# Self-attention's product of folded values and turned probabilities, as three products of rounded parts in three of four groups

## The reference

```python
b, sq, _ = x.shape                       # 2, 128; 4 groups of 4 heads, 128 wide
q = jnp.einsum('bsh,he->bse', x, w_q).reshape(b, sq, GROUPS, HPG, KVC)
kv = jnp.einsum('bsh,he->bse', x, w_kv)
k, v = jnp.split(kv, 2, axis=-1)         # one key and one value head a group
scores = jnp.einsum('bqgpd,bkgd->bgqpk', q, k) * (SCALE / LAYER_INDEX)
scores = jnp.where(causal[None, None, :, None, :], scores, -jnp.inf)
probs = jax.nn.softmax(scores, axis=-1).astype(x.dtype)
ctx = jnp.einsum('bgqpk,bkgd->bqgpd', probs, v).reshape(b, sq, HEADS * KVC)
return jnp.einsum('bse,eh->bsh', ctx, w_dense)
```

## Time and profile before

| | |
|---|---|
| Median of 3 runs | 344.44 us (344.17 to 345.36) |
| The profiled execution's own time | 344.5 us |
| Its span, first to last instruction | 342.7 us |
| Granted TensorE clock, mean | 1.000 |
| Busy: PE, DVE | 328.6 us (96%), 270.5 us (79%) |
| Busy: ACT, POOL | 228.9 us (67%), 220.7 us (64%) |

### The profile page before, as it was taken

The page is one execution under the profiler, slowest core; times in us unless marked ns, Lnnn a source line. Parts: engine busy times, 40 slices in busy tenths (PEclk is TensorE's granted clock), DMA queues, the critical chain, the costliest instruction groups (busy, mean ns, idle before and its releaser), DMA issues.

```text
span 342.7 us, 6810 instructions
## 1 busy us (share of the span) xinstructions
PE 328.6 (96%) x2222; PEld 297.3 (87%) x2222; DVE 270.5 (79%) x466; ACT 228.9 (67%) x410; POOL 220.7 (64%) x136
## 2 busy tenths in 40 slices
PE   6999988999999999999999999899999999899995
PEld 5887867999999999999999988899888897699994
DVE  2776888898988989889889889577559746489996
ACT  3799449577687677777777676874155676266771
POOL 3766709799499599499598686924626773117540
PEclk9999999999999999999999999999999999999999
DMA  6811468876886895895875977994043054005630
GB/s 201 253 33 38 91 158 191 207 178 142 224 202 138 204 207 124 208 203 127 204 179 115 202 179 175 212 294 137 2 135 112 0 155 153 4 0 138 175 102 32
DMA packets 32565, 49.98 MB, mean 146 GB/s; under 512 B 5536, under 2 KB 23072, under 8 KB 32544
## 3 DMA queue, kind: packets, MB, share of 16 engines
q1 hardware_dynamic: 32544, 49.72, 57.8%
HBM read 20.08 MB, written 0.26 MB: 59 GB/s over the span
## 4 chain that ended last, share of the span: by engine, by line
PE 81%; DVE 6%; ACT 4%; SPq 3%; issue 2%; POOL 1%; DMA 1%; DVEq 0%; POOLq 0%; ACTq 0%
PE bank L586 12%; PE bank L587 11%; PE bank L588 11%; PE pair L586 10%; PE pair L588 10%; PE pair L587 10%; SPq L284 3%; PE bank L977 2%; PE bank L790 2%; PE bank L1007 1%; ACT probs L1248 1%; PE pair L970 1%; PE bank L970 1%; ACT first_pT L1320 1%; PE pair L936 1%
## 5 line engine op out<-in xcount | busy, mean ns | idle before, releaser
L455 POOL TENSOR_TENSOR pT<-pT,pT_hi 128x1024 fp32r<-128x1024 f32 x54 | 129.5, 2422 | 35.5 <-ACT pT_hi L1258 35.4
L1248 ACT ACTIVATE probs<-probs,lowest 128x2048 f32<-128x2048 f32 x32 | 64.4, 2012 | 23.3 <-DVE lowest L1640 23.3
L1258 ACT ACTIVATE pT_hi<-pT 128x1024 fp32r<-128x1024 f32 x56 | 57.6, 1055 | 13.0 <-DMA pT<-ctx_raw 8.6
L586 PE MATMUL bank<-pT_hi,ctx_lo 128*128 128x256 f32 x224 | 63.9, 285 | 1.2 <-POOL pT L455 1.2
L587 PE MATMUL bank<-pT,ctx_hi 128*128 128x256 f32 x224 | 64.1, 286 | 0.0
L588 PE MATMUL bank<-pT_hi,ctx_hi 128*128 128x256 f32 x224 | 63.5, 284 | 0.0
L586 PE MATMUL pair<-ctxT_hi,qk_lo 128*128 128x512 f32 x128 | 52.2, 408 | 0.0
L588 PE MATMUL pair<-ctxT_hi,qk_hi 128*128 128x512 f32 x128 | 50.1, 391 | 0.0
L587 PE MATMUL pair<-ctxT_lo,qk_hi 128*128 128x512 f32 x128 | 50.0, 391 | 0.0
L1640 DVE CUSTOM_DVE_ANT_0 probs<-pair,mask_bias,lowest 128x1024 f32<-128x1024 f32 x32 | 41.0, 1280 | 10.7 <-PE pair L588 10.1
L455 POOL TENSOR_TENSOR ctx_lo<-ctx_raw,ctx_hi 128x512 fp32r<-128x512 f32 (+1 forms) x19 | 31.4, 1668 | 23.0 <-DVE route L2028 8.5
(11 more groups left out here) (280 smaller groups left out, 793.5 us busy)
## 6 DMA issues: line engine op xcount, KB each, us to landing
pT<-blocks SPq DMA_DIRECT2D x112, 128.0 KB, 2.3
pT<-ctx_raw SPq DMA_DIRECT2D x112, 128.0 KB, 2.3
ctx_raw<-ffn_experts_gate_up_dram SPq DMA_DIRECT2D x16, 256.0 KB, 2.9
wq<-in_L_xattn_Wq_dram SPq DMA_DIRECT2D x8, 256.0 KB, 2.7
ctx_raw<-in_ctx_dram SPq DMA_DIRECT2D x8, 256.0 KB, 6.7
wo<-in_L_xattn_Wo_dram SPq DMA_DIRECT2D x8, 256.0 KB, 2.9
blocks<-in_L_attn_w_dense_dram SPq DMA_DIRECT2D x4, 512.0 KB, 4.9
ctx_raw<-_L_ffn_experts_down_dram SPq DMA_DIRECT2D x16, 128.0 KB, 2.5
```

Source lines behind the costliest of these rows:

```text
L455: pool.tensor_tensor(dst, src, hi.bitcast(F32), ALU.subtract).then_inc(ready, 1)
L586: pe.matmul(dst, w[1], x[0], start=start, stop=False)
L1248: act.activation(probs[:, j], probs[:, j], ACT.Exp, bias=lowest[:, p, j, 1:2], scale=-1.0, accum_out=den[:, p, j:j + 1]).then_inc(exps, 1)
L1258: act.activation(hi_slot(c), chunk(p, c).bitcast(F32), ACT.Copy).then_inc(pT_hi_ready, 1)
```

## The change

In groups 0, 1 and 2 the product of `attend2` is done by `product`, with operands in two parts each. The parts lie in tiles that are not in use at that stage (`p2T`'s in `wq_hi`, `wo_hi`, `wq_lo`, `wo_lo`, `v2`'s in `qT_hi`, `qT_lo`). ACT's copy of the turned probabilities writes the rounded part instead of the float32 tile; a new function `rest_p2T` on DVE subtracts it from PC[b] for the low part. DVE's `copy_v` writes a rounded part, waits for it, and subtracts. `rest_p2T(r - 1, b)` stands in DVE's queue ahead of `scale2(r, b)`. In group 3 the product stays as it was.

```diff
--- before.py
+++ after.py
@@ -175,6 +175,9 @@
         v2 = work[:, 1280:1536].rearrange("p (b d) -> p b d", b=B)
         p2 = work[:, 1536:2560].rearrange("p (b h k) -> p b h k", b=B, h=HR)
         p2T = work[:, 2560:3584].rearrange("p (b n) -> p b n", b=B)
+        p2T_hi = (wq_hi[:].rearrange("p k e -> p (k e)"), wo_hi[:].rearrange("p j n -> p (j n)"))
+        p2T_lo = (wq_lo[:].rearrange("p k e -> p (k e)"), wo_lo[:].rearrange("p j n -> p (j n)"))
+        v2_hi, v2_lo = (v[:, 0:B * P].rearrange("p (b d) -> p b d", b=B) for v in (qT_hi, qT_lo))
         nm2 = work[:, 3584:3592].rearrange("p (b h) -> p b h", b=B)
         ds2 = work[:, 3600:3608].rearrange("p (b h) -> p b h", b=B)
         rd2 = work[:, 3616:3624].rearrange("p (b h) -> p b h", b=B)
@@ -277,6 +280,7 @@
         gu_psum, silu_ready, h_ready, down_psum, added3 = (
             sem("gu_psum"), sem("silu_ready"), sem("h_ready"), sem("down_psum"), sem("added3"))
         stored = sem("stored")
+        p2T_hi_ready, v2_hi_ready = sem("p2T_hi_ready"), sem("v2_hi_ready")
         xn_half, half_stat = sem("xn_half"), sem("half_stat")
 
         def move(eng, p, a, q):
@@ -974,7 +978,11 @@
             def attend2(r, b):
                 pe.wait_ge(v2_ready, r + 1)
                 pe.wait_ge(p2T_ready, 2 * r + b + 1)
-                pe.matmul(PC[b][:], v2[:, b], p2T[:, b], start=True, stop=True).then_inc(c2_psum, 1)
+                if r == R - 1:
+                    last = pe.matmul(PC[b][:], v2[:, b], p2T[:, b], start=True, stop=True)
+                else:
+                    last = product(PC[b][:], (v2_hi[:, b], v2_lo[:, b]), (p2T_hi[b], p2T_lo[b]), True, True)
+                last.then_inc(c2_psum, 1)
 
             def dense2(r):
                 pe.wait_ge(wd2_ready, r + 1)
@@ -1481,7 +1489,7 @@
                 for b in range(B):
 
                     act.wait_ge(p2T_psum, 2 * r + b + 1)
-                    act.activation(p2T[:, b], PC[b][:], ACT.Copy).then_inc(p2T_ready, 1)
+                    act.activation(p2T_hi[b], PC[b][:], ACT.Copy).then_inc(p2T_hi_ready, 1)
 
             def whole_rows(b):
                 act.wait_ge(xnT_psum, B + b + 1)
@@ -1866,7 +1874,19 @@
 
                 after(dve, c2_psum, 2 * r)
                 dve.wait_ge(k2_ready, r + 1)
-                dve.tensor_copy(v2.rearrange("p b d -> p (b d)"), KV[:, B * P:2 * B * P]).then_inc(v2_ready, 1)
+                src = KV[:, B * P:2 * B * P]
+                if r == R - 1:
+                    dve.tensor_copy(v2.rearrange("p b d -> p (b d)"), src).then_inc(v2_ready, 1)
+                else:
+                    dve.tensor_copy(v2_hi.rearrange("p b d -> p (b d)"), src).then_inc(v2_hi_ready, 1)
+                    dve.wait_ge(v2_hi_ready, r + 1)
+                    dve.tensor_tensor(v2_lo.rearrange("p b d -> p (b d)"), src,
+                                      v2_hi.rearrange("p b d -> p (b d)").bitcast(F32),
+                                      ALU.subtract).then_inc(v2_ready, 1)
+
+            def rest_p2T(r, b):
+                dve.wait_ge(p2T_hi_ready, 2 * r + b + 1)
+                dve.tensor_tensor(p2T_lo[b], PC[b][:], p2T_hi[b].bitcast(F32), ALU.subtract).then_inc(p2T_ready, 1)
 
             def rest_c(r):
                 for b in range(B):
@@ -1885,6 +1905,8 @@
 
             def group2(r, before, split):
                 for b in range(0 if before else 1, B):
+                    if before:
+                        rest_p2T(r - 1, b)
                     scale2(r, b)
                     max2(r, b)
                 copy_v(r)
@@ -1909,6 +1931,7 @@
 
             def last_group2():
                 for b in range(B):
+                    rest_p2T(R - 2, b)
                     scale2(R - 1, b)
                     max2(R - 1, b)
                 invert(R - 1, 0)
```

## The result

The changed kernel takes 347.56 us (median of 4 runs, 347.23 to 349.14), the kernel before 344.39 (4 runs). The ratio is 1.0086, with an interval of [1.0063, 1.0109]: about 3 us slower, as forecast (347.5). The profiled execution has a span of 345.5 us and a time of 347.24, which is 2.74 above the 344.5 of the profiled execution before.

A forecast was written before the change was run, and what follows sets the result against it. PE was taken to bound the kernel, busy for 96% of the span. Terms of 1.78, 0.95, 0.2 and 0.05 sum to +2.98 us on 344.5, giving 347.5 us; range 345.8 to 348.9.

The forecast's parts named there:

- The product's own price: Six of eight attend2 products on PE: three parts take 0.69 us instead of 0.86, saving 0.17 each, 1.02 together.
- Group 1, +1.78: Group r = 1: PE, waiting for DVE's second subtraction, is free at 264.03 instead of 262.25, +1.78 us.
- Group 2, +0.95: Group r = 2: PE is free later by +1.11 us, or +0.76 if DVE's first rounding shortens; +0.95 taken.
- Last group, +0.2: Last group: second subtraction delays DVE's normalisation and the copy behind it by 0.19, keeping PE: +0.2 us, bounds 0.2 and 0.4.
- Folded values, +0.05: copy_v's added subtraction costs DVE 0.45 us in three groups; +0.05 shows in r = 0, hidden in r = 1 and 2.
- Sum: Whole kernel: 1.78 + 0.95 + 0.2 + 0.05 = +2.98 us, the saved 1.02 included in these differences.
- The signs: Expected in the profile after: PE idle about 0.9 and 1.2 us in r = 1, 0.2 and 1.2 in r = 2; clock unchanged.
- Rival 1: In r = 1 DVE's copy starts before POOL and takes 0.28: +0.35 instead of +1.78, total 346.4 us; chance 0.14.
- Rival 2: POOL also holds DVE's new subtractions, in r = 2: up to 2.4 us more, 349 to 350 us; chance 0.06.
- Rival 4: Nothing measurable: PE is late but gets it back behind, 344.5 to 345.5 us; chance 0.07.
- Rival 3: Faster: the subtractions are in time and PE keeps its saved 1.02 us, 343.5 us; chance 0.05.

The follow-up runs named there:

- the control: Kernel before, with ACT copying raw value weights after group 0, copy_c ahead of exps2(r, 0), rest_c ahead of copy_v: 345.17 us, ratio 1.0013.

## Why the prediction was right

- **The product's own price.** 0.17 us less each, from rows. Measured: three starts 0.23 apart, and 0.77 instead of 0.69 for a product that starts out of a wait (263.71 to 264.48), because 0.31 then lies between its first two starts.
- **Group 1, +1.78.** Measured +1.86. The anchor (DVE's copy of 2.44 us) held: it was repeated to the hundredth, and taking the copy from DVE took 1.37 us back. The gap of 0.1 from DVE to PE was 0.15 (263.56 to 263.71). With it and the longer product PE is free 1.92 later, and the 0.07 that it waited ahead of the dense product in the kernel before (at 265.08) is gone.
- **Group 2, +0.95**, between 0.76 and 1.11. Measured +0.92. The reason given for the lower bound came true in full: the first rounding took 0.30 at 272.00 instead of 0.62. That alone gives about 0.8; the rest is what the sum had left out, 0.04 of hand-over from DVE to PE and 0.09 of product. So the middle value was hit because two errors cancel.
- **Last group, +0.2.** Measured +0.19. The second product ends 0.5 later after the mark than before, and 0.3 of that disappears ahead of the dense product behind the turn, which starts 0.27 after the end of DVE's copy of the context in both kernels (287.90 to 288.17, 291.19 to 291.46). It is the path that the prediction named.
- **Folded values, +0.05.** The subtraction takes 0.42 us, and what follows starts 0.45 later, as priced. POOL's normalisations of r = 0 end 1.51 us after the first mark instead of 1.46, and PE's scores behind the turn start at 2.05 instead of 2.02, so what reaches PE is 0.03; it lies in the stage of group 1 above. In r = 1 it is hidden, as the kernel without `rest_p2T` shows.
- **Sum**, +2.98 against +2.97 by the stages and 3.2 by the medians. They are this close partly by luck: group 2 was hit by two errors that cancel, and the start and the end of one execution differ from those of another by 0.3 to 0.5 us, which is more than the sum is off.
- **The signs.** PE's idle times were forecast as 0.9 and 1.2 us in r = 1, and the brackets say 0.76 and 0.99. The forecast is from start to start, the brackets count from a record's end, which lies 0.16 to 0.17 later; in starts they are 0.93 and 1.15. In r = 2 no wait of 0.2 came before the first product, since the rounding was short. The granted clock stayed at 1.00, as said.
- **Rival 1** did not come about; POOL still started 0.11 before the copy (258.50 and 258.61). Its priced value for a free DVE, +0.35 in group 1, compares with +0.49 when ACT made the copy. **Rival 2** did not either: `rest_p2T` took 0.68 at 273.57 and 0.69 at 285.67 while POOL was at work. **Rival 4** did not: behind the last mark everything stays 3.26 late.
- **What it had wrong.** Rival 3's price. It gave the 1.02 us of PE to a kernel in which the subtractions are in time. The kernel without them, whose products are faster still, kept 0.0 of 0.8 us in r = 1, 0.60 in r = 2 and nothing in the last group: the dense product and the turn of group 3 took it back. The prediction looked at the wait that the change adds, and did not ask what stood 3 us behind it on the same engine at nearly zero slack. It is in part by this that the first repair (both subtractions first) gave 0.7 us instead of 2.5; the longer rounding in r = 2 and the later softmax of the last group took 0.3 each.

## What to carry to other kernels

Price an added subtraction by its place in the queue of the engine that makes it: in group 1 two subtractions of 0.7 us cost 1.9 us of PE, since the second was fourth in a queue that itself began late. Before counting on a faster product, list every later point of the same group at which that engine waits for the slower one and how much each has in hand; repairing the first shows the second. And an engine that runs ahead by its own chain (POOL here) can be moved out of the way by one wait, if its work is not due.

## What the runs showed of the hardware

- A DVE instruction with two float32 inputs in SBUF (128 x 512) took 1.54 us beside a POOL subtraction and 0.69 without; a subtraction of the same size with one input in PSUM took 0.68 to 0.69 beside POOL in every group. DVE's SBUF-to-SBUF copy of 256 elements took 0.28 or 2.44.
- Gaps of up to 1 us in PE's work left the granted clock at 1.00 in the profiled execution of the changed kernel. It is not so in every execution. In the profiled ones of both kernels PE is idle for 1.07 us some 8 us behind the last mark, before it turns the norm's rows, and the clock stays at 1.00. In the profiled execution of the control PE has the same gap (it ends at 298.84), and the clock is 1.00 up to 300 us and 0.50, the level of 1.2 GHz, from 301 to 304; matmuls of 256 columns start 0.21 us apart there instead of 0.12. From the last mark to the experts' row it takes 47.42 us instead of 46.71. The three stages lie ahead of this, at 1.00 in every kernel here.
- Over the runs, executions of the kernel before had mean clocks from 0.992 to 1.000, and those near 0.994 took about 1 us longer (345.5 against 344.5, medians of 8 and 12 in one series). The changed kernel had such executions too, two of four, and its two at 1.000 took 347.2.
